# The second norm's weight multiplied into the weights' rows, with a reordered queue

## The chip, the cores and the metric

The kernel runs as one program on one core of one Trainium2 chip. The metric is the device time of the whole program in microseconds; it is given as the median of several runs. The change is compared with the kernel before it, on the same inputs.

## The reference

The input x has 32 batches of 128 channels by 512 positions; ctx has the same shape.

```
x = x + tanh(g_xattn) * cross_attention(layernorm(x), ctx, Wq, bq, Wk, bk, Wv, bv)   # 8 heads of 16
x = x + tanh(g_ffn)   * ffn(layernorm(x))

ffn(x):  h = rmsnorm(x) * rms_weight             # rms_weight: 512 values, one per feature
         probs = softmax(h @ router_w); two best of 8 experts, renormalised
         moe = sum over the two of weight * (silu(h @ w_gate) * (h @ w_up)) @ w_down
         sh  = (silu(h @ sw_gate) * (h @ sw_up)) @ sw_down
         return moe + sh
```

A batch's 128 rows of 512 are its 128 tokens in the second part. rms_weight meets h only in products over the 512 features: the router's, and the gate and up products of the eight experts and of the shared one.

## The kernel before, in words

**First part, attention, in turns.** `TURNS` runs from -3 to 31. Each engine has its own list of the turns' work, written out by hand, and within a turn TensorE, VectorE and ScalarE work through 32 slots (`STEPS`). In turn i the exponentials of batch i are made (TensorE: `exp_scores`, line 878; ScalarE: `exponential`, line 1395; TensorE: `values`, line 907), and beside them the maxima of batch i+1 (TensorE: `max_scores`, line 857; VectorE: `maximum`, line 1123, two matmuls' results to one reduction of 1.2 us). The maxima of half a batch are turned by TensorE (`turn_maxima`, line 866), taken by VectorE (`maxima_rows`, lines 1132 and 1133) and written by a DMA into one row of the q stack (`row`, line 531), from which the scores of `exp_scores` take them. The first scores of a batch need the row of half 0, its scores from slot 16 on the row of half 1.

Products of q and k are made from three bf16 parts each. ScalarE makes the high part, GpSimd the middle and low one (`split`, lines 677 to 680); SyncE writes each part to DRAM (`write`, line 456, DMAs to `parts_k` and `parts_q`) and reads them back stacked (`read`, line 470, six DMAs for each of k and q). The maxima of batch i+2 need both reads, made in turn i.

The values' result carries the denominators. Per turn, SyncE spreads them (line 486), stores the result (479), VectorE inverts them (`invert`, line 1115, in slot `RECIP_AT` = 11), SyncE stores the reciprocals (490) and, when these have landed, loads both spread out again (`load_values`, 497 and 498), and GpSimd adds the attention to x (`add_attention`, 687 to 689).

GpSimd then normalises the batch for the second part (`tokens`, line 717: scale and shift; line 718: times `w_rms`, the norm's weight broadcast to 128 partitions) and SyncE stores it to DRAM. TensorE turns it and makes the router's logits; VectorE chooses the experts; GpSimd scatters token numbers to a map by indirect DMA (`scatter`, line 733).

In turns -2 to 27 one of 30 rows of expert weights is staged per turn: loaded (`load_staged`), its high part rounded by ScalarE (`staged_high`, line 1417), its low part made by GpSimd (`staged_low`, line 725), both stored (`store_staged`). Rows 0 to 3 of an expert (or of the shared one) are gate and up weights of 128 features each, rows 4 and 5 down weights.

SyncE's order in one turn: write high q part, row of half 1, denominators, result, read k, write q parts, store reciprocals, load ctx, store turned tokens, row of half 0, read q, load values, store tokens, load x, store staged, load staged, write the three k parts. A wait in it holds all that follows.

**Second part, jobs.** From about 931 us on, 32 jobs of the shared expert and 71 routed jobs (128 gathered tokens each) run, each of which TensorE does as three products of high and low parts (line 950). Rows of the shared expert are split by VectorE in the last turn (`shared_parts`, lines 1217 and 1218), those of experts 0 to 2 beside the jobs (`placed_high`, line 1453; `placed_low`, line 1301).

Lines 1526 to 1532 set up the arrays; the rms weight is passed (line 1530) as one row of 512.

Of the kernel before, what the change touches and what calls it, by code (L numbers as in the profile page):

```python
# [15 lines left out]
P = 128  # L16
HEADS = 8
DH = P // HEADS
L = 512
# [46 lines left out]
RECIP_AT = 11  # L66
# [39 lines left out]
def build(nc, x_d, ctx_d, g_xattn_d, g_ffn_d, wq_d, bq_d, wk_d, bk_d, wv_d, bv_d, rms_d, router_d, w_d, out_d):  # L106
# [6 lines left out]
    with es:  # L113
# [62 lines left out]
        w_rms = a.take(L)  # L176

        routed_act = [w_rms[:, n * FF:(n + 1) * FF] for n in range(2)]
# [50 lines left out]
        w_router = sb("w_router", [P, CHUNKS, EXPERTS])  # L229
        before = sb("before", [P, P], BF16)  # L230
# [166 lines left out]
        n_const = 4  # L397
# [18 lines left out]
        def _(sp):  # L416
# [28 lines left out]
            load(wv[:], wv_d)  # L445
            for b in range(1, X_AHEAD - 3):
                load_x(b)
# [86 lines left out]
            for i in TURNS:  # L534
# [11 lines left out]
                if is_b(i - 1):  # L546
                    store_reciprocals(i - 1)
                if is_b(i + 4) and i + 4 >= 2:
                    load_ctx(i + 4)
                if is_b(i - 3):  # L550
                    store_turned(i - 3)
                if is_b(i + 1):
                    row(i + 1, 0)
                if is_b(i + 2):
                    read(i + 2, 1)
# [4 lines left out]
                if is_b(i + X_AHEAD):  # L560
                    load_x(i + X_AHEAD)
                if 0 <= i + 2 < len(STAGED):
                    store_staged(i + 2)
                if 0 <= i + 3 < len(STAGED):
                    load_staged(i + 3)
                if is_b(i + 3):
                    for part in (HI, MID, LO):
                        write(i + 3, 0, part)
# [12 lines left out]
                if i == 0:  # L581
                    sp.dma_start(w_router[:], router_d.rearrange("(c p) e -> p c e", p=P)).then_inc(s_wnorm, DMA)
                    sp.dma_start(w_rms, rms_d.broadcast_to([P, L])).then_inc(s_wnorm, DMA)
# [57 lines left out]
        def _(pool):  # L641
# [64 lines left out]
            def tokens(b):  # L706
# [5 lines left out]
                if b:  # L712
                    pool.wait_ge(s_tr, b)
                    pool.wait_ge(s_hst, DMA * (b + 1))
                else:
                    pool.wait_ge(s_wnorm, 2 * DMA)
                link(nc.gpsimd.tensor_scalar(tok, xs[:, b, :], r, nmr2[:, b:b + 1], ALU.mult, ALU.add))
                nc.gpsimd.tensor_tensor(tok, tok, w_rms, ALU.mult).then_inc(s_h, 1)
                pool.wait_ge(s_h, b + 1)

            def staged_low(k):
                pool.wait_ge(s_sh, k + 1)
                if k:
                    pool.wait_ge(s_sst, 2 * DMA * k)
                nc.gpsimd.tensor_tensor(staged[LOW][:], staged_raw, staged[HI][:].bitcast(F32), ALU.subtract
                                        ).then_inc(s_sl, 1)
# [19 lines left out]
            for i in TURNS:  # L746
# [6 lines left out]
                if 0 <= i + 2 < len(STAGED):  # L753
                    staged_low(i + 2)
                for b in range(B - 2 * CHUNK):
                    if i == min(b + 10, B - 1):
                        scatter(b)
                if is_b(i + 3) and i + 3 > 0:
# [52 lines left out]
        def _(pe):  # L811
# [174 lines left out]
            for i in TURNS:  # L986
                for s in range(0, STEPS, GROUP):
# [12 lines left out]
                    if is_b(i):  # L1000
                        exp_scores(i, s + 2)
                        exp_scores(i, s + 3)
                    if s == 0 and is_b(i - 1):
# [3 lines left out]
                    if s + 3 == MAX_AT[1] and is_b(i):  # L1007
                        turn_maxima(i, 1)
                    if s + 3 == MAX_AT[0] and is_b(i + 1):
                        turn_maxima(i + 1, 0)  # L1010
# [28 lines left out]
        def _(dve):  # L1039
# [172 lines left out]
            def shared_parts(r):  # L1212
                dve.wait_ge(s_wsh, W_ROWS * DMA)
                if r == 0:
                    dve.wait_ge(s_part, 4 * B)
                return chain(
# [82 lines left out]
            def placed_low(e, r):  # L1299
                dve.wait_ge(s_ph, W_ROWS * e + r + 1)  # L1300
                nc.vector.tensor_tensor(w_ring[:, e, LOW, r, :], raw_expert[:, r, :], w_ring[:, e, HI, r, :].bitcast(F32),
                                        ALU.subtract).then_inc(s_wrt, 1)
# [66 lines left out]
        def _(act_e):  # L1369
# [42 lines left out]
            def staged_high(k):  # L1412
# [4 lines left out]
                nc.scalar.copy(staged[HI][:], staged_raw).then_inc(s_sh, 1)  # L1417
# [30 lines left out]
            def placed_high(e, r):  # L1448
# [4 lines left out]
                nc.scalar.copy(w_ring[:, e, HI, r, :], raw_expert[:, r, :]).then_inc(s_ph, 1)  # L1453
# [87 lines left out]
```

## Time and profile before

| | |
|---|---|
| median of 3 runs | 1432.28 us |
| lowest, highest | 1427.72, 1443.97 us |
| the profiled execution | 1418.35 us, its span 1416.5 us |
| mean granted TensorE clock in it | 0.979 of full speed |
| busy in it: PE, VectorE, ScalarE, GpSimd | 1333.9, 984.4, 872.6, 868.1 us |
| DMA | 247.90 MB, mean 175 GB/s |

PE is TensorE, DVE is VectorE, ACT ScalarE, POOL GpSimd, SP or SPq SyncE and its queue. Instructions run one after the other on each engine; "idle before" is the time that an engine stood still ahead of an instruction, and the name behind the arrow is what it then waited for. A line stands for a place in the kernel. In order of time, a row gives start, length, engine, line, operation, what is written from what, the count, and in brackets the idle time.

### The profile page before, as it was taken

The numbers are of one execution on the slowest core, as the hardware profiler recorded it, in microseconds if no ns is written. First come the engines' busy times: TensorE is split into PE (matmuls) and PEld (weight loads), VectorE is DVE, ScalarE is ACT, GpSimd is POOL, SyncE is SP. The second block draws the span as 40 slices with busy tenths as digits, with TensorE's granted clock in tenths as the row PEclk, the third lists the DMA queues.
The fourth block names the chain that finished last, engine by engine and source line by source line (L and its number), as shares of the span: only waits on it lengthen the run. The fifth ranks groups of instructions, "written<-read, shape, count | busy, mean of one in ns | idle before, by whom it ended". The sixth has DMA issues, their size and how long they took to land.

```text
span 1416.5 us, 24632 instructions
## 1 busy us (share of the span) xinstructions
PE 1333.9 (94%) x7290; PEld 648.6 (46%) x7290; DVE 984.4 (69%) x1661; ACT 872.6 (62%) x1720; POOL 868.1 (61%) x1278
## 2 busy tenths in 40 slices
PE   3899999999999999999999998899999999999997
PEld 1222223222222322222232232377787888888886
DVE  4888889998798988988899988556654333333332
ACT  2488788788687877777787886724334333333433
POOL 7447667768687877777788864542213555555553
PEclk8799999999999999999999999999999999999999
DMA  6567676676676767676766763366554788786655
GB/s 174 159 183 220 188 215 210 187 208 198 170 192 196 200 180 193 214 182 178 200 205 188 196 181 104 101 218 154 136 186 81 195 217 207 175 198 110 114 106 81
DMA packets 161309, 247.90 MB, mean 175 GB/s; under 512 B 33605, under 2 KB 58828, under 8 KB 161182
## 3 DMA queue, kind: packets, MB, share of 16 engines
q1 hardware_dynamic: 142926, 208.96, 51.6%
q0 software_dynamic: 18256, 37.38, 14.2%
q8 instruction: 64, 1.05, 0.3%
q14 instruction: 63, 0.52, 0.1%
HBM read 141.32 MB, written 103.88 MB: 173 GB/s over the span
## 4 chain that ended last, share of the span: by engine, by line
PE 61%; DVE 13%; issue 10%; DMA 6%; SPq 4%; POOL 3%; POOLq 1%; ACT 1%; DVEq 0%; ACTq 0%
PE m_banks L950 20%; PE bank L907 12%; PE bank L878 11%; DVE row_max L1123 9%; PE m_banks L857 7%; PE bank L838 4%; PE bank L894 2%; DMA arena<-parts_q 2%; DMA arena<-arena 2%; PE bank L883 2%; PE bank L842 2%; POOL xs L781 2%; SPq L470 2%; SPq L531 1%; PE bank L972 1%
## 5 line engine op out<-in xcount | busy, mean ns | idle before, releaser
L1123 DVE TENSOR_REDUCE row_max<-m_banks 128x2 f32<-128x1024 f32 x512 | 614.6, 1222 | 68.9 <-PE m_banks L857 63.5
L1395 ACT ACTIVATE arena<-bank 128x512 f32<-128x512 f32 x1024 | 556.2, 606 | 101.7 <-PE bank L878 96.9
L878 PE MATMUL bank<-arena 112*128 112x512 bf16 x1024 | 314.8, 386 | 2.4 <-ACT arena L1395 1.5
L907 PE MATMUL bank<-arena 128*32 128x512 f32 x2048 | 277.3, 613 | 0.4 <-ACT arena L1403 0.4
L793 POOL DMA_INDIRECT out<-xs,ids x71 | 112.5, 1584 | 172.9 <-ACT xs L1470 137.9
L857 PE MATMUL m_banks<-arena 48*128 48x512 bf16 x1024 | 169.9, 393 | 47.1 <-DVE row_max L1123 34.6
L878 PEld LDWEIGHTS bank<-arena 112*128 112x128 bf16 x1024 | 79.7, 100 | 247.0 <-ACT arena L1395 88.5
L950 PE MATMUL m_banks<-w_ring,h_hi 128*128 x568 | 183.1, 403 | 0.0
L1459 ACT ACTIVATE arena<-m_banks 128x256 f32<-128x256 f32 x103 | 39.5, 384 | 188.7 <-PE m_banks L950 188.6
L857 PEld LDWEIGHTS m_banks<-arena 48*128 48x128 bf16 x1024 | 39.8, 93 | 185.2 <-issue 87.2
L950 PE MATMUL m_banks<-w_ring,h_lo 128*128 x284 | 111.7, 393 | 0.0
L1319 DVE TENSOR_TENSOR arena<-arena,m_banks 128x256 f32<-128x256 f32 x71 | 29.9, 421 | 117.0 <-ACT arena L1459 117.0
L677 POOL TENSOR_TENSOR arena<-arena 128x512 bf16<-128x512 f32 x62 | 71.8, 1157 | 63.5 <-ACT arena L1387 60.4
L950 PEld LDWEIGHTS m_banks<-w_ring,h_hi 128*128 128x128 f32 x568 | 101.4, 189 | 18.4
L687 POOL TENSOR_TENSOR arena<-arena 128x512 f32<-128x512 f32 x32 | 40.7, 1272 | 98.5 <-DMA arena<-pv_d 95.5
L1313 DVE TENSOR_TENSOR act_lo<-bank,act_hi 128x256 fp32r<-128x256 f32 x71 | 30.1, 424 | 96.7 <-ACT act_hi L1476 96.7
L781 POOL DMA_INDIRECT xs<-h_d,ids x71 | 69.7, 982 | 41.4 <-issue 21.0
L733 POOL DMA_INDIRECT map_d<-meta,slots x64 | 66.4, 1038 | 44.6 <-DVE slots L1210 28.3
L838 PE MATMUL bank<-arena 128*128 128x512 f32 x128 | 76.9, 684 | 16.8 <-POOL arena L668 12.0
L1470 ACT ACTIVATE xs<-m_banks,wts 128x512 f32<-128x512 f32 x71 | 48.8, 688 | 71.1 <-PE m_banks L950 71.1
L1378 ACT ACTIVATE arena<-bank,bias 128x512 f32<-128x512 f32 x64 | 44.0, 687 | 76.7 <-PE bank L838 76.7
L950 PE MATMUL m_banks<-w_ring,act_hi 128*128 x284 | 87.6, 390 | 1.4 <-DVE act_lo L1313 1.4
(176 smaller groups left out, 2047.9 us busy)
## 6 DMA issues: line engine op xcount, KB each, us to landing
pv_d<-arena SPq DMA_DIRECT2D x32, 512.0 KB, 4.3
w_ring<-split_d SPq DMA_DIRECT2D x60, 256.0 KB, 3.9
parts_k<-arena SPq DMA_DIRECT2D x96, 128.0 KB
parts_q<-arena SPq DMA_DIRECT2D x96, 128.0 KB
arena<-parts_k SPq DMA_DIRECT2D x64, 192.0 KB
arena<-parts_q SPq DMA_DIRECT2D x64, 192.0 KB
arena<-in_w SPq DMA_DIRECT2D x36, 256.0 KB, 7.0
arena<-in_ctx SPq DMA_DIRECT2D x32, 256.0 KB, 3.4
```

The source lines that it names most:

```text
L677: nc.gpsimd.tensor_tensor(mid, proj[n], hi, ALU.subtract).then_inc(s_part, 1)
L733: nc.gpsimd.indirect_dma_start(map_d, bass.IndirectOffsetOnAxis(ap=slots[:, k, b:b + 1], axis=0), meta[:, k, b, :], None).then_inc(s_sc2, DMA)
L781: nc.gpsimd.indirect_dma_start(gathered[i % IN_RING], None, h_d, bass.IndirectOffsetOnAxis(ap=ids[:, i:i + 1], axis=0)).then_inc(s_got[i % ...
L793: nc.gpsimd.indirect_dma_start(out_d, bass.IndirectOffsetOnAxis(ap=ids[:, i:i + 1], axis=0), y_sb[i % OUT_RING], None, compute_op=ALU.add) ...
L838: nc.tensor.matmul(out, (wk, wq)[n][:], ctx_in[b % 2] if n == 0 else xn[b % 2], start=True, stop=True).then_inc(s_proj, 1)
L857: nc.tensor.matmul(m_ps[pair % M_PAIRS][:, a, :], q_stack[b % 3][rows, h, qt * P:(qt + 1) * P], k_stack[b % 3][rows, h, :], start=True, st ...
L878: nc.tensor.matmul(out, k_stack[b % 3][0:SHIFTED, h, kt * P:(kt + 1) * P], q_stack[b % 3][0:SHIFTED, h, :], start=True, stop=True).then_in ...
L907: last = nc.tensor.matmul(pv_ps[2 * DH * j:2 * DH * (j + 1), :], v_ones[b % 3][:, kt, GROUP * g + j, :], probs[pair % 3][:, j, :], start=( ...
L950: last = nc.tensor.matmul(out, v[:, c, :], weights(j, part, first_row + c), start=(c == 0 and n == 0), stop=(c == chunks - 1 and n == 2))
L1123: nc.vector.reduce_max(pair, m_ps[(STEPS * b + u) // 2 % M_PAIRS], AX_X).then_inc(s_mx, 1)
L1395: nc.scalar.activation(probs[group % 3][:, j, :], bank_of["scores", b, s], ACT.Exp, scale=float(DH) ** -0.5).then_inc(s_exp, 1)
L1470: nc.scalar.activation(y_sb[i % OUT_RING], Y_PS[j % 2], ACT.Copy, scale=wts[:, i:i + 1]).then_inc(s_yrt, 1)
```

## The change

The norm's weight is loaded at the start as 128 x 4 values, feature by partition, in place of a broadcast of 512 to all partitions in turn 0. GpSimd no longer multiplies the tokens by it; it multiplies the router's weights once. The gate and up rows (0 to 3) get the factor where their high and low parts are made: staged rows by ScalarE (a multiply in place of a copy) and GpSimd (one more instruction, in place, ahead of the subtraction), shared and placed rows in forms of the same instructions with a second operand. Rows 4 and 5 are as before. So the tokens in DRAM are without the weight.

Beside it the order changes. On SyncE the read of q goes ahead of the store of reciprocals and of the row of half 0, and the high k part is written ahead of the staged parts. On GpSimd the scatters go ahead of the staged low part. On TensorE `turn_maxima` goes ahead of `values` in its slots. On VectorE the reciprocals move from slot 11 to slot 16.

```diff
--- before.py
+++ after.py
@@ -63,7 +63,7 @@
 LOGITS_AT = 16
 MOMENTS2_AT = 10
 MOMENTS_AT = 27
-RECIP_AT = 11
+RECIP_AT = 16
 GROUP = 4
 EXPERTS = 8
 FF = 256
@@ -173,9 +173,7 @@
         added_all = a.take(NT + 1)
         a.take(2 * L - NT * EXPERTS - NT - 1)
         assert a.at >= attention_end, (a.at, attention_end)
-        w_rms = a.take(L)
-
-        routed_act = [w_rms[:, n * FF:(n + 1) * FF] for n in range(2)]
+        routed_act = [a.take(FF) for _ in range(2)]
 
 
 
@@ -227,6 +225,7 @@
         nmr2 = sb("nmr2", [P, B])
         newton = sb("newton", [P, 1])
         w_router = sb("w_router", [P, CHUNKS, EXPERTS])
+        w_rms = sb("w_rms", [P, CHUNKS])
         before = sb("before", [P, P], BF16)
         ones = sb("ones", [P, P], BF16)
         route = sb("route", [P, 12 * C])
@@ -394,7 +393,7 @@
         MOMENTS_JOB = 6
         TURN_AT = 24
 
-        n_const = 4
+        n_const = 5
         TURNS = range(-3, B)
 
         ROUTER_JOBS = {0: B - 3, 4: B - 2, 9: B - 1}
@@ -443,6 +442,7 @@
             load(gates[:, 0:1], g_xattn_d.broadcast_to([P, 1]))
             load(gates[:, 1:2], g_ffn_d.broadcast_to([P, 1]))
             load(wv[:], wv_d)
+            load(w_rms[:], rms_d)
             for b in range(1, X_AHEAD - 3):
                 load_x(b)
 
@@ -543,29 +543,31 @@
                     read(i + 2, 0)
                     write(i + 2, 1, MID)
                     write(i + 2, 1, LO)
-                if is_b(i - 1):
-                    store_reciprocals(i - 1)
                 if is_b(i + 4) and i + 4 >= 2:
                     load_ctx(i + 4)
                 if is_b(i - 3):
                     store_turned(i - 3)
+                if is_b(i + 2):
+                    read(i + 2, 1)
+                if is_b(i - 1):
+                    store_reciprocals(i - 1)
                 if is_b(i + 1):
                     row(i + 1, 0)
-                if is_b(i + 2):
-                    read(i + 2, 1)
                 if is_b(i - 1):
                     load_values(i - 1)
                 if is_b(i - 2):
                     store_tokens(i - 2)
                 if is_b(i + X_AHEAD):
                     load_x(i + X_AHEAD)
+                if is_b(i + 3):
+                    write(i + 3, 0, HI)
                 if 0 <= i + 2 < len(STAGED):
                     store_staged(i + 2)
                 if 0 <= i + 3 < len(STAGED):
                     load_staged(i + 3)
                 if is_b(i + 3):
-                    for part in (HI, MID, LO):
-                        write(i + 3, 0, part)
+                    write(i + 3, 0, MID)
+                    write(i + 3, 0, LO)
                 for r in SHARED_ROWS.get(i, ()):
                     if r == 2:
                         sp.wait_ge(s_sst, 2 * DMA * len(STAGED))
@@ -580,7 +582,6 @@
                     sp.dma_start(map_tiles[EXPERTS * B:], unused_map).then_inc(s_map0, DMA)
                 if i == 0:
                     sp.dma_start(w_router[:], router_d.rearrange("(c p) e -> p c e", p=P)).then_inc(s_wnorm, DMA)
-                    sp.dma_start(w_rms, rms_d.broadcast_to([P, L])).then_inc(s_wnorm, DMA)
 
 
             def load_expert(e, r):
@@ -713,15 +714,20 @@
                     pool.wait_ge(s_tr, b)
                     pool.wait_ge(s_hst, DMA * (b + 1))
                 else:
-                    pool.wait_ge(s_wnorm, 2 * DMA)
-                link(nc.gpsimd.tensor_scalar(tok, xs[:, b, :], r, nmr2[:, b:b + 1], ALU.mult, ALU.add))
-                nc.gpsimd.tensor_tensor(tok, tok, w_rms, ALU.mult).then_inc(s_h, 1)
+                    pool.wait_ge(s_wnorm, DMA)
+                    pool.wait_ge(s_const, n_const * DMA)
+                    link(nc.gpsimd.tensor_tensor(w_router[:], w_router[:],
+                                                 w_rms[:].unsqueeze(2).broadcast_to([P, CHUNKS, EXPERTS]), ALU.mult))
+                nc.gpsimd.tensor_scalar(tok, xs[:, b, :], r, nmr2[:, b:b + 1], ALU.mult, ALU.add).then_inc(s_h, 1)
                 pool.wait_ge(s_h, b + 1)
 
             def staged_low(k):
                 pool.wait_ge(s_sh, k + 1)
                 if k:
                     pool.wait_ge(s_sst, 2 * DMA * k)
+                r = STAGED[k][1]
+                if r < CHUNKS:
+                    link(nc.gpsimd.tensor_scalar(staged_raw, staged_raw, w_rms[:, r:r + 1], None, ALU.mult))
                 nc.gpsimd.tensor_tensor(staged[LOW][:], staged_raw, staged[HI][:].bitcast(F32), ALU.subtract
                                         ).then_inc(s_sl, 1)
 
@@ -750,11 +756,11 @@
                     normalise(i + 4)
                 if is_b(i - 2):
                     tokens(i - 2)
-                if 0 <= i + 2 < len(STAGED):
-                    staged_low(i + 2)
                 for b in range(B - 2 * CHUNK):
                     if i == min(b + 10, B - 1):
                         scatter(b)
+                if 0 <= i + 2 < len(STAGED):
+                    staged_low(i + 2)
                 if is_b(i + 3) and i + 3 > 0:
                     split(i + 3, 0)
                 if is_b(i - 1):
@@ -1000,14 +1006,14 @@
                     if is_b(i):
                         exp_scores(i, s + 2)
                         exp_scores(i, s + 3)
+                    if s + 3 == MAX_AT[1] and is_b(i):
+                        turn_maxima(i, 1)
+                    if s + 3 == MAX_AT[0] and is_b(i + 1):
+                        turn_maxima(i + 1, 0)
                     if s == 0 and is_b(i - 1):
                         values(i - 1, STEPS // GROUP - 1)
                     if s and is_b(i):
                         values(i, s // GROUP - 1)
-                    if s + 3 == MAX_AT[1] and is_b(i):
-                        turn_maxima(i, 1)
-                    if s + 3 == MAX_AT[0] and is_b(i + 1):
-                        turn_maxima(i + 1, 0)
                     if s + 3 == COUNT_SLOT and i >= 7 and (i - 7) % CHUNK == 0:
                         count_choices((i - 7) // CHUNK)
                     if i == B - 1 and s == FIRST_JOB_AT:
@@ -1213,6 +1219,13 @@
                 dve.wait_ge(s_wsh, W_ROWS * DMA)
                 if r == 0:
                     dve.wait_ge(s_part, 4 * B)
+                if r < CHUNKS:
+                    return chain(
+                        lambda: nc.vector.tensor_scalar(shared_hi[:, r, :], w_shared[:, r, :], w_rms[:, r:r + 1], None,
+                                                        ALU.mult),
+                        lambda: nc.vector.scalar_tensor_tensor(shared_lo[:, r, :], w_shared[:, r, :], w_rms[:, r:r + 1],
+                                                               shared_hi[:, r, :].bitcast(F32), ALU.mult, ALU.subtract
+                                                               ).then_inc(s_wsp, 1))
                 return chain(
                     lambda: nc.vector.tensor_copy(shared_hi[:, r, :], w_shared[:, r, :]),
                     lambda: nc.vector.tensor_tensor(shared_lo[:, r, :], w_shared[:, r, :],
@@ -1298,8 +1311,13 @@
 
             def placed_low(e, r):
                 dve.wait_ge(s_ph, W_ROWS * e + r + 1)
-                nc.vector.tensor_tensor(w_ring[:, e, LOW, r, :], raw_expert[:, r, :], w_ring[:, e, HI, r, :].bitcast(F32),
-                                        ALU.subtract).then_inc(s_wrt, 1)
+                hi = w_ring[:, e, HI, r, :].bitcast(F32)
+                if r < CHUNKS:
+                    nc.vector.scalar_tensor_tensor(w_ring[:, e, LOW, r, :], raw_expert[:, r, :], w_rms[:, r:r + 1], hi,
+                                                   ALU.mult, ALU.subtract).then_inc(s_wrt, 1)
+                else:
+                    nc.vector.tensor_tensor(w_ring[:, e, LOW, r, :], raw_expert[:, r, :], hi, ALU.subtract
+                                            ).then_inc(s_wrt, 1)
 
             def tokens_low(j):
                 hi, lo = (flat(v) for v in tokens_of(j))
@@ -1414,7 +1432,11 @@
                 if k:
                     act_e.wait_ge(s_sl, k)
                     act_e.wait_ge(s_sst, 2 * DMA * k)
-                nc.scalar.copy(staged[HI][:], staged_raw).then_inc(s_sh, 1)
+                r = STAGED[k][1]
+                if r < CHUNKS:
+                    nc.scalar.mul(staged[HI][:], staged_raw, w_rms[:, r:r + 1]).then_inc(s_sh, 1)
+                else:
+                    nc.scalar.copy(staged[HI][:], staged_raw).then_inc(s_sh, 1)
 
             def exponentials(c):
                 act_e.wait_ge(s_ch, c + 1)
@@ -1450,7 +1472,10 @@
                     act_e.wait_ge(s_praw, DMA * W_ROWS * (e + 1))
                 if e == IN_PLACE - 1:
                     act_e.wait_ge(s_dn, B)
-                nc.scalar.copy(w_ring[:, e, HI, r, :], raw_expert[:, r, :]).then_inc(s_ph, 1)
+                if r < CHUNKS:
+                    nc.scalar.mul(w_ring[:, e, HI, r, :], raw_expert[:, r, :], w_rms[:, r:r + 1]).then_inc(s_ph, 1)
+                else:
+                    nc.scalar.copy(w_ring[:, e, HI, r, :], raw_expert[:, r, :]).then_inc(s_ph, 1)
 
             def silu(j):
                 act_e.wait_ge(s_gu, j + 1)
@@ -1527,7 +1552,7 @@
     arrays = dict(
         x=x, ctx=inputs["ctx_2048"], g_xattn=inputs["g_xattn"].reshape(1, 1), g_ffn=inputs["g_ffn"].reshape(1, 1),
         wq=attention("Wq").T, bq=attention("bq").reshape(P, 1), wk=attention("Wk").T, bk=attention("bk").reshape(P, 1),
-        wv=attention("Wv").T, bv=attention("bv").reshape(P, 1), rms=ffn("rms_weight").reshape(1, L),
+        wv=attention("Wv").T, bv=attention("bv").reshape(P, 1), rms=ffn("rms_weight").reshape(CHUNKS, P).T,
         router=ffn("router_w"), w=weights.transpose(0, 2, 1, 3))
     arrays = {f"in_{name}": np.ascontiguousarray(value) for name, value in arrays.items()}
     tokens = x.shape[0] * P
```

## Rows read from the trace of the kernel before

**Rows 1.** Busy by stage: PE, PEld, DVE, ACT, POOL; clock, DMA share, GB/s.

```profile
110.00:890.00 780.00, 745.99 (x4409) 218.87 (x4408) 683.92 (x1070) 609.78 (x1171) 570.50 (x953) 0.99 0.68 191
890.00:931.00 41.00, 34.82 (x186) 17.18 (x184) 22.64 (x60) 24.06 (x47) 23.41 (x36) 0.96 0.41 125
1060.00:1416.00 356.00, 346.40 (x1727) 287.01 (x1725) 114.94 (x225) 133.91 (x293) 177.43 (x137) 0.99 0.69 148
```

**Rows 2.** The page, the chain that ended last, by engine.

```profile
PE 61%; DVE 13%; issue 10%; DMA 6%; SPq 4%; POOL 3%; POOLq 1%; ACT 1%; DVEq 0%; ACTq 0%
```

**Rows 3.** Busy time by engine in single turns, columns as in the first group.

```profile
537.20:564.80 27.60, 26.00 (x159) 7.68 (x155) 23.78 (x40) 21.42 (x42) 21.53 (x37) 1.00 0.71 193
730.80:756.80 26.00, 25.69 (x159) 7.79 (x155) 24.16 (x39) 21.35 (x42) 21.11 (x36) 1.00 0.72 208
```

**Rows 4.** Waits of TensorE from 53 to 890 us: total, times, longest.

```profile
PE m_banks L857 <- DVE row_max L1123: 28.4, 47, 1.4
PE m_banks L857 <- DMA arena<-parts_q: 6.0, 4, 2.1
```

**Rows 5.** Waits of VectorE from 53 to 890 us.

```profile
DVE m_rows L1132 <- PE bank L866: 14.6, 30, 1.5
DVE arena L1115 <- issue: 13.7, 8, 2.7
DVE arena L1115 <- DVE stats L1088: 2.4, 4, 1.0
```

**Rows 6.** Chain of waits, 545 to 553 us: start, length, what.

```profile
543.10 3.56 DMA arena<-arena
546.66 1.77 issue
```

**Rows 7.** TensorE in order of time, two instructions of two turns.

```profile
551.65 0.39 PE L857 MATMUL m_banks<-arena 48*128 48x512 bf16 x2 [1.12 <-DVE row_max L1123]
425.83 0.60 PE L878 MATMUL bank<-arena 112*128 112x512 bf16 x2
```

**Rows 8.** Waits of SyncE's queue from 53 to 890 us.

```profile
SPq L531 <- DVE m_rows L1133: 101.6, 58, 6.2
```

**Rows 9.** Chain of waits at the start, issue to landing.

```profile
21.60 3.83 DMA parts_q<-arena
50.68 4.18 DMA arena<-parts_q
```

**Rows 10.** SyncE's queue in order of time, parts of two turns.

```profile
413.44 1.33 SPq L456 DMA_DIRECT2D parts_q<-arena  x2
...
416.37 1.22 SPq L531 DMA_DIRECT2D arena<-m_rows  x2
418.08 3.76 SPq L470 DMA_DIRECT2D arena<-parts_q  x6
421.95 0.63 SPq L497 DMA_DIRECT2D arena<-rden_d  x1
...
435.38 3.81 SPq L470 DMA_DIRECT2D arena<-parts_k  x6
...
774.67 3.77 SPq L470 DMA_DIRECT2D arena<-parts_q  x6
...
790.32 3.80 SPq L470 DMA_DIRECT2D arena<-parts_k  x6
```

**Rows 11.** GpSimd by line, 110 to 890 us: busy, mean ns, idle before.

```profile
L718 POOL TENSOR_TENSOR arena<-arena 128x512 f32<-128x512 f32 x29 | 37.1, 1280 | 2.4
L687 POOL TENSOR_TENSOR arena<-arena 128x512 f32<-128x512 f32 x29 | 36.9, 1271 | 79.8 <-DMA arena<-pv_d 79.8
L717 POOL TENSOR_SCALAR arena<-xs,r,nmr 128x512 f32<-128x512 f32 x29 | 22.4, 774 | 2.9
```

**Rows 12.** The store of reciprocals, line 490, to landing.

```profile
DMA to landing us min/median/max: 1.4/3.1/4.2
```

**Rows 13.** One group of ScalarE by line, 110 to 890 us.

```profile
L1417 ACT CAST staged_hi<-arena 128x512 fp32r<-128x512 f32 x26 | 16.3, 629 | 0.0
```

## The prediction

> **What bounds the kernel now.** I read the view by stages first. From 110 to 890 us the attention turns run: TensorE is busy 746.0 of 780 us, VectorE 683.9, ScalarE 609.8, GpSimd 570.5; from 1060 us on, in the routed jobs, TensorE is busy 346.4 of 356 us and nobody else is near [rows 1]. The chain that ended last says the same: PE 61%, DVE 13% [rows 2]. The change touches nothing that TensorE computes, so it can only win TensorE's idle time, and of that there are some 34 us in the turns and 10 us behind them. A turn takes 780/29 = 26.9 us on average (29 is the count of line 687, once a turn [rows 11]).
>
> Next, single turns. One without a stall takes 26.0 us with TensorE busy 25.7; one with a stall takes 27.6 with TensorE busy 26.0 [rows 3]. The list of waits names the two causes: TensorE waits 28.4 us (47 times) in the maxima's matmuls for VectorE's reductions and 6.0 us (4 times) for the reads of the q parts [rows 4]. VectorE's own waits, one level deeper: 13.7 + 2.4 us (12 times) before the reciprocal of line 1115 and 14.6 us (30 times) before line 1132, which takes the turned maxima [rows 5]. The chain of one stalled turn shows the link: the denominators are in flight for 3.56 us, VectorE waits 1.77 us in front of its reciprocal, and TensorE then idles 1.12 us for the reduction queued behind it [rows 6, 7]. So of such a wait 1.12/1.77 = 0.63 reaches TensorE.
>
> Last, SyncE's queue, because the change mostly permutes it. It waits 101.6 us (58 times) for the rows of maxima [rows 8], with the reads of the q parts queued behind.
>
> **The change, part by part.**
>
> Reciprocal moved from slot 11 to 16 of VectorE's order: 16.1 us of waiting go, worth 16.1 x 0.63 = 10 us. Bounds: 0 (the reductions wait for TensorE anyway) and 16. The stores that need it were moved behind the reads, so its lateness costs nothing.
>
> Turning of maxima ahead of the value products on TensorE: the transpose runs about 1 us sooner (a group of value products), so VectorE's 14.6 us before line 1132 go. VectorE then mostly meets the next wait for TensorE, so I take 3 us; bounds 0 and 14.6 x 0.63 = 9. The value products start 0.28 us later; their reader on ScalarE comes a slot later.
>
> Reads of the q parts ahead of reciprocals and rows: their data are there earlier. The last q part is issued at about 414.1 (second of the pair at 413.44), and such a write lands 3.83 us after issue [rows 9], at 417.9; the reads start at 418.08, behind the rows issued at 416.37 [rows 10]. In the turn at 790.32 the pair is issued from 794.2 on, that is 790.32 + 3.80, and would have landed by 798.7, while the waits for maxima [rows 8] hold the queue 1 to 2 us. The 6.0 us of TensorE's waits for these reads should go: 5 us; bounds 0 and 6. Sum of these three: 10 + 3 + 5 = 18 us off, if nothing else becomes late.
>
> GpSimd: line 718 goes, 1.28 us a turn; one tensor_scalar like line 717, 0.77 us, comes for four of six staged rows [rows 11]. Net 0.4 us less per such turn, 1.3 otherwise. Worth nothing: GpSimd already idles 79.8 us before line 687 waiting for the loaded values [rows 11], and this cover stays. Scatters ahead of the staged part: the store of the staged low half may be 2 us later, but SyncE gets there later too. ScalarE multiplying in place of copying, 0.63 us each [rows 13]: at worst the few hundredths of a scale operand, and ScalarE is idle 170 us of 780 [rows 1]. The shared rows' two-operand forms on VectorE: a few tenths each, four times, in a stretch where it is busy 22.6 of 41 us [rows 1]. The placed rows: VectorE and ScalarE are busy under 40% of the routed jobs [rows 1]. Weight load: one small issue moved to the start behind wv and the x of batch 0, a broadcast gone later: nothing. One 128x32 multiply on GpSimd, once: nothing.
>
> **What the permuted queue costs.** The store of reciprocals now follows the six reads, and loading values waits for that store. The store of tokens, the load of x, the first k part and the staged parts stand behind that wait; GpSimd's addition of attention, and later ScalarE's staged row in slot 15, wait for what they bring. Before, values were issued 3.87 us after the reads began (421.95 against 418.08 [rows 10]), their bytes queued behind the reads' without a gap. Now follow one lap of the queue's own loop. The six reads take 3.8 us to issue and the last lands 4.18 us after its issue [rows 9]: all landed at +7.4. The reciprocals, issued at +3.9, pass behind them: taken as landed with the reads at +7.4. Then load_values is issued, and the DMA engines have run dry: a gap of 1.4 us, the smallest time to landing of this store [rows 12], for I found no purer row; bounds 0.5 and its median 3.1. Then the burst (values, tokens, x, staged halves, weights, k parts), until the k parts have landed and their reads start: from 418.08 + 7.4 = 425.5 to 435.38, 9.9 us, and from 774.67 + 7.4 to 790.32, 8.2 us [rows 10]; I take 9.1. Then the six k reads (3.8), the two q parts (issue of the last at +0.7) and its landing (3.83): 8.35. Sum 7.4 + 1.4 + 9.1 + 8.35 = 26.3 us; bounds 24.5 and 28.8. TensorE without the 18 us would turn in 26.9 - 18/29 = 26.3 us. A tie: each turn takes the later of two paces that both vary, so I take 26.6, that is 0.3 x 29 = 9 us of the 18 given back. The first wait to show it would be the first row of maxima of a batch: issued behind reads, reciprocals and at +4.5 it lands about +7.5 to +8.5, while in the tight turn the scores need it 7.75 us after the reads begin (425.83 [rows 7] against 418.08 [rows 10]).
>
> The Trainium skill (DMA: Bandwidth & Descriptors, "Queues, rings and completion order") says that one issuer's descriptors are taken in ring order and that the semaphore increment lands only after every earlier write of that DMA engine. By that rule a small store behind six reads cannot signal before them, which speaks against this order; with its page's fixed 2 us in place of 1.4 the lap would be 26.9, an estimate by that page. The trace neither contradicts nor isolates it.
>
> **Rivals.** (a) TensorE alone sets the pace: the lap closes in 26 us or less (shorter gap, or the burst at 8.2), and all 18 us stay, perhaps 22 with more of line 1132. Time 1432 - 20 = 1412. For it: the k reads already wait at the queue, so the burst may fill in; half of the staged traffic is unchanged. Chance 0.36. (b) Slower: the reciprocals' store behind the reads delays load_values by 2 us and more each turn; the lap becomes 27.6 (midway from 26.3 to the upper bound 28.8), SyncE's late row of maxima stops TensorE before the first scores of each turn, +0.7 x 29 = +20 us, 1452. It decides once the lap passes 27.4 (26.9 and 14 us spread over 29 turns). For it: DMA engines are busy 0.7 of these turns [rows 3], the tight turn has 0.3 us of slack. Chance 0.22. (c) The stall only moves: VectorE now waits in front of line 1088 for x that GpSimd adds after the later values, and nothing changes: 1430, part of the forecast's side.
>
> **How the numbers follow.** The profiled execution took 1418.35 us (span 1416.5); the runs shown have median 1432.28 (1427.72 to 1443.97), so it lies 1% below them. My forecast, -9 us, gives 1409 against its own time and 1423 against the median, which is the number I give. What a measurement of this kernel can tell from no change is about 1%, 14 us. Forecast with (c): 0.42, all of it within 1%. Faster by over 1%: (a), 0.36. Slower by over 1%: (b), 0.22. The forecast's own range is 1418 to 1436, the lap between 26.1 and 26.8 and (c). The whole range reaches down to 1404, which is (a) with bounds of its terms (16 + 6 + 6 = 28 us off), and up to 1450, about (b)'s middle; what is left out is the upper half of (b), up to 1487 where the lap is at its bound of 28.8 ((28.8 - 26.9) x 29 = 55 us), and a small tail of (a), together under 2 in 10.
>
> **What would show it.** Right: no idle before line 1115 (now 12 waits) and next to none before 1132; no wait of TensorE for the q parts; SyncE's wait for maxima much shorter and a new wait for the reciprocals' store in front of load_values of 1.5 to 2.5 us a turn; unstalled turns at 26.3 to 26.6. (a) if turns are 26.0 to 26.3. (b) if TensorE's line 878 waits for the DMA of m_rows. Wrong altogether if the routed jobs, 346.4 us of TensorE, change, since nothing there should.

## The result, and the profile after

Slower: 1487.72 us median (1480.6 to 1490.2, 4 runs) against 1430.0 (1426.54 to 1443.97, 4 runs), ratio 1.038, 95% interval 1.030 to 1.046. The profiled execution took 1480.6 us, span 1478.7, with a mean granted TensorE clock of 0.964 (before 0.979). I had forecast 1423 and a range up to 1450. What came is the second rival, and the time at the bound that the prediction had left out (1487, for a lap of 28.8 us; the laps in the trace are longer, see below).

The page's chain that ended last, by engine, where PE and DVE stood first before [rows 2]:

```profile
DMA 32%; SPq 26%; PE 23%; issue 10%; POOL 3%; DVE 3%; ACT 1%; POOLq 1%; ACTq 0%
```

So on this chain SyncE's queue and the transfers that it waits for come first. Line numbers have shifted: in the kernel after, `exp_scores` is line 884, `max_scores` 863, `maximum` 1129, `invert` 1121, `add_attention` 688; SyncE's 470 to 531 are as before. First the stages, columns as in [rows 1]; the second row is the same stretch of routed jobs, reckoned from the end:

```profile
110.00:890.00 780.00, 715.43 (x4097) 203.11 (x4093) 628.01 (x998) 574.27 (x1093) 535.10 (x903) 0.96 0.63 180
1122.00:1478.00 356.00, 345.33 (x1717) 285.10 (x1715) 114.00 (x222) 133.83 (x291) 177.46 (x137) 1.00 0.69 148
```

The routed jobs are untouched (345.3 of 356 us, before 346.4 [rows 1]). The loss lies in the turns: TensorE's busy time in 780 us fell from 746.0 to 715.4, its clock from 0.99 to 0.96, the share of the DMA engines from 0.68 to 0.63. All engines do less per microsecond. Both windows lie inside the turns, which end some 60 us later than before.

The waits of TensorE from 53 to 890 us (total, times, longest), to be held against [rows 4]:

```profile
PE bank L884 <- DMA arena<-m_rows: 52.2, 35, 4.2
PE m_banks L863 <- DVE row_max L1129: 10.4, 33, 1.0
```

The waits that the change aimed at did shrink: for VectorE's reductions from 28.4 to 10.4 us, for the q parts from 6.0 to none. A new one is larger than both: the scores wait for the row of maxima. VectorE (against [rows 5]) no longer waits before the reciprocal or before the turned maxima, but it waits for its inputs and, a little, for x:

```profile
DVE row_max L1129 <- PE m_banks L863: 129.5, 143, 5.3
DVE stats L1094 <- POOL xs L690: 16.4, 15, 1.8
```

And SyncE's queue in the same stretch (against [rows 8]):

```profile
SPq L497 <- DMA rden_d<-arena: 75.9, 27, 4.7
SPq L470 <- DMA parts_q<-arena: 57.6, 29, 2.4
SPq L470 <- DMA parts_k<-arena: 44.6, 26, 2.3
```

Its wait for the rows of maxima, 101.6 us before, is down to 1.2: the rows are ready when SyncE comes to them, because SyncE comes late. In its place stands a wait of 2.8 us a turn at line 497, `load_values`, for the reciprocals' store. SyncE's waits for engines are 4 us in all now, beside 178 us for transfers: the queue waits for its own DMAs.

One lap in order of time (start, length, line, what, count), against [rows 10]:

```profile
407.21 3.77 SPq L470 DMA_DIRECT2D arena<-parts_q  x6
411.02 0.59 SPq L490 DMA_DIRECT2D rden_d<-arena  x1
411.66 1.18 SPq L531 DMA_DIRECT2D arena<-m_rows  x2
415.71 0.66 SPq L497 DMA_DIRECT2D arena<-rden_d  x1
...
420.90 1.25 SPq L456 DMA_DIRECT2D parts_k<-arena  x2
...
427.95 3.81 SPq L470 DMA_DIRECT2D arena<-parts_k  x6
431.80 1.33 SPq L456 DMA_DIRECT2D parts_q<-arena  x2
...
436.05 1.23 SPq L470 DMA_DIRECT2D arena<-parts_q  x2
```

From one set of q reads to the next it is 436.05 - 407.21 = 28.8 us. The store is issued 3.8 us after the reads begin, and 4.7 us pass before `load_values` may go, at +8.5; before it went at +3.9 [rows 10]. The two rows of maxima, issued from 411.66 on, are under way behind the reads, and TensorE stands:

```profile
416.93 0.86 PE L884 MATMUL bank<-arena 112*128 112x512 bf16 x2 [2.71 <-DMA arena<-m_rows]
```

The lap shown is shorter than most. Over the 23 laps from batch 6 on, start of q reads to start of q reads, the mean is 29.5 us, against 27.2 before: 2.3 x 29 turns = 65 us, and the spans differ by 62. Split into the same three stretches (26 laps that begin between 110 and 870 us), the means are 8.9 us to `load_values`, at most 10.4, then 12.3 to the k reads and 8.3 to the next q reads.

### The profile page after: what moved, and what is told of

Same layout as the page of the kernel before. It is cut to its first block, busy times and chain, and to the rows that moved or that the text cites. A ratio compares the mean times of both kernels' runs of the same rounds, so it can differ in the third digit from the quotient of the medians.

```text
span 1478.7 us, 24638 instructions
## 1 busy us (share of the span) xinstructions
PE 1361.0 (92%) x7290; PEld 646.5 (44%) x7290; DVE 975.4 (66%) x1661; ACT 881.0 (60%) x1720; POOL 855.5 (58%) x1267
## 4 chain that ended last, share of the span: by engine, by line
DMA 32%; SPq 26%; PE 23%; issue 10%; POOL 3%; DVE 3%; ACT 1%; POOLq 1%; ACTq 0%
PE m_banks L956 17%; SPq L470 15%; DMA parts_k<-arena 12%; DMA rden_d<-arena 10%; DMA parts_q<-arena 7%; SPq L456 4%; SPq L520 2%; POOL xs L787 2%; DMA out<-xs,ids 2%; DVE row_max L1129 2%; SPq L497 1%; PE bank L913 1%; SPq L514 1%; SPq L498 1%; PE bank L889 1%
## 5 line engine op out<-in xcount | busy, mean ns | idle before, releaser
L884 PE MATMUL bank<-arena 112*128 112x512 bf16 x1024 | 321.4, 396 | 55.9 <-DMA arena<-m_rows 53.6
L913 PE MATMUL bank<-arena 128*32 128x512 f32 x2048 | 282.2, 623 | 0.3 <-ACT arena L1421 0.3
L884 PEld LDWEIGHTS bank<-arena 112*128 112x128 bf16 x1024 | 72.4, 101 | 363.0 <-ACT arena L1413 138.8
L863 PE MATMUL m_banks<-arena 48*128 48x512 bf16 x1024 | 174.4, 402 | 27.2 <-DVE row_max L1129 21.0
L1331 DVE TENSOR_TENSOR act_lo<-bank,act_hi 128x256 fp32r<-128x256 f32 x71 | 30.1, 424 | 96.5 <-ACT act_hi L1501 96.5
L844 PE MATMUL bank<-arena 128*128 128x512 f32 x128 | 77.3, 688 | 17.0 <-POOL arena L669 12.3
```

The lines of the kernel that those rows point to most:

```text
L844: nc.tensor.matmul(out, (wk, wq)[n][:], ctx_in[b % 2] if n == 0 else xn[b % 2], start=True, stop=True).then_inc(s_proj, 1)
L863: nc.tensor.matmul(m_ps[pair % M_PAIRS][:, a, :], q_stack[b % 3][rows, h, qt * P:(qt + 1) * P], k_stack[b % 3][rows, h, :], start=True, st ...
L884: nc.tensor.matmul(out, k_stack[b % 3][0:SHIFTED, h, kt * P:(kt + 1) * P], q_stack[b % 3][0:SHIFTED, h, :], start=True, stop=True).then_in ...
L913: last = nc.tensor.matmul(pv_ps[2 * DH * j:2 * DH * (j + 1), :], v_ones[b % 3][:, kt, GROUP * g + j, :], probs[pair % 3][:, j, :], start=( ...
```

## The experiments

The fold is the norm's weight multiplied into the weights' rows. Theory L: SyncE's lap, lengthened by the reciprocals' store behind the reads, is the whole loss. Rival R: the row of maxima behind the reads stops TensorE. Rival F: the fold costs. The runs come in three sets of four, in the order below, each on another chip. All ratios are against the kernel before on the same chip, where it took 1449.87, 1445.56 and 1447.4 us, with a 95% interval in brackets. No trace of the kernel before belongs to these sets: its rows are of the execution of 1418.35 us. Where a wait of a run is held against [rows 4], [rows 5] or [rows 8], a part of the difference can be the chip's.

**The fold alone.**

```diff
 after.py, with all orders and RECIP_AT = 11 as before
```

> The weight goes into the weights' rows as in the changed kernel; all orders (SyncE, GpSimd, TensorE, slot 11 of the reciprocals) are those of before. Theory L (the lap of SyncE's queue, lengthened by the reciprocals' store behind the reads, is the whole loss): 0 to 4 us under before, 1426 to 1430, turns of 26.9 us. Rival F (the folding itself costs, through ScalarE's multiplies, GpSimd's extra instruction or VectorE's two-operand forms): 1450 or more.

Measured 1.003 (0.999 to 1.007), 1450.42 us. The fold is free within what can be told; it wins nothing either, as costed. F falls. This kernel has VectorE's order of before, and shows more waiting ahead of the reciprocal than [rows 5], 30.4 us in place of 16.1 (53 to 890 us):

```profile
DVE arena L1119 <- issue: 22.8, 13, 3.4
DVE arena L1119 <- DMA arena<-arena: 4.3, 2, 2.2
DVE arena L1119 <- DVE stats L1092: 3.3, 6, 0.8
```

**The reordering alone.**

```diff
 before.py, with SyncE's, GpSimd's and TensorE's orders of after and
-RECIP_AT = 11
+RECIP_AT = 16
```

> The reordering alone, tokens multiplied by the weight as before. Theory L: the whole loss is here, ratio 1.03 to 1.045 (1475 to 1492), SyncE waits 75 to 90 us for the reciprocals' store ahead of line 497's like. Rival F: near before.

Measured 1.030 (1.022 to 1.038), 1492.14 us; SyncE waits 79.6 us at line 497 from 53 to 890 us (86.4 up to 950). The loss is in the order.

**The changed kernel, the store put back.**

```diff
+                if is_b(i - 1):
+                    store_reciprocals(i - 1)
                 if is_b(i + 4) and i + 4 >= 2:
                     load_ctx(i + 4)
 ...
                 if is_b(i + 2):
                     read(i + 2, 1)
-                if is_b(i - 1):
-                    store_reciprocals(i - 1)
                 if is_b(i + 1):
                     row(i + 1, 0)
```

> The changed kernel with one step undone: the store of reciprocals goes back ahead of the load of ctx; the row of half 0 stays behind the reads of q. Theory L: load_values is issued 5.1 us after the reads begin in place of 8.5 to 9.5, the lap falls from 29.5 to about 26.7, time 1420 to 1436, and TensorE's wait for the rows of maxima falls under 10 us. Rival R (it is the row of maxima behind the six reads that stops TensorE): TensorE still waits about 50 us for m_rows and the time stays over 1465.

Measured 0.998 (0.994 to 1.002), 1445.69 us. This one step takes back the whole loss; of the 18 us that were to be won nothing is seen clear of noise, and the lap is 28.2 us in the mean, not 26.7. TensorE still waits 22.6 us for rows of maxima (53 to 950 us), more than the 10 that I had written, less than half of R's 50. SyncE now waits for the reciprocal itself (53 to 890 us):

```profile
SPq L490 <- DVE arena L1121: 58.1, 27, 3.6
SPq L531 <- DVE m_rows L1139: 52.5, 26, 4.1
```

**The changed kernel, the row put back.**

```diff
+                if is_b(i + 1):
+                    row(i + 1, 0)
                 if is_b(i + 2):
                     read(i + 2, 1)
                 if is_b(i - 1):
                     store_reciprocals(i - 1)
-                if is_b(i + 1):
-                    row(i + 1, 0)
```

> The changed kernel with the other step undone: the row of half 0 goes back ahead of the reads of q; the store of reciprocals stays behind them. Theory L: load_values still waits for that store, the lap stays at 28.8 to 30, time 1475 to 1500, with TensorE's waits for m_rows replaced by waits for the q reads. Rival R: the row is in time, the waits are gone, 1445 or less.

Measured 1.042 (1.034 to 1.051), 1511.77 us. R said 1445 or less, and falls. My detail was off: TensorE's waits for rows did not vanish (line 884 from 53 to 950 us), they moved:

```profile
PE bank L884 <- DMA arena<-m_rows: 40.2, 21, 3.8
PE m_banks L863 <- DMA arena<-parts_q: 19.1, 13, 3.3
```

Counted by slot, all 40 us now lie before slot 16, that is before the row of half 1, which SyncE issues early in the next turn; in the changed kernel 46 of 53 us (53 to 950 us) lay before slot 0, the row of half 0. With the row moved forward TensorE waits for another row and for q parts, and the loss stays: where it waits is a symptom of the late queue.

**Slot 16 alone, in the kernel before.**

```diff
-RECIP_AT = 11
+RECIP_AT = 16
```

> The kernel before with the reciprocals in slot 16 of VectorE's order and nothing else. The prediction's term of 10 us: ratio 0.993 or less if SyncE, which now waits for the reciprocal ahead of its store, does so only in time that it spent on the next row of maxima anyway. Rival (seen in the run with the store put back, where SyncE waited 69 us there): that wait delays the reads of q, TensorE then waits for them, ratio 1.00 or above. VectorE's idle time before the reciprocal goes to 0 in both.

Measured 0.981 (0.975 to 0.986), 1419.28 us against 1445.56. This is the lowest ratio of the study, below the kernel before and the changed one: some 27 us (20 to 36 by the interval) for one number. The wait that could have eaten it is there, 29.1 us (18 times) at SyncE's line 490 from 53 to 890 us, and seems to lie in time that SyncE spent on the maxima before (50.5 us left of 101.6 [rows 8]). TensorE's waits for the q parts, the expectation's rival, are 12.2 us (6 times), against 6.0 [rows 4]. VectorE's list from 53 to 890 us has no reciprocal any more (against [rows 5]):

```profile
DVE row_max L1123 <- PE m_banks L857: 69.2, 154, 4.6
DVE m_rows L1132 <- PE bank L866: 8.6, 30, 1.3
DVE stats L1088 <- POOL xs L689: 3.7, 3, 1.6
```

**turn_maxima first, in the kernel before.**

```diff
+                    if s + 3 == MAX_AT[1] and is_b(i):
+                        turn_maxima(i, 1)
+                    if s + 3 == MAX_AT[0] and is_b(i + 1):
+                        turn_maxima(i + 1, 0)
                     if s == 0 and is_b(i - 1):
                         values(i - 1, STEPS // GROUP - 1)
 ...
```

> The kernel before with turn_maxima ahead of values on TensorE and nothing else. The prediction's term of 3 us, bounds 0 and 9: ratio 0.994 to 1.000, VectorE's idle time before line 1132 gone. Rival: TensorE waits for a free bank of scores with the transpose in front, ratio above 1.000.

Measured 0.988 (0.982 to 0.994), 1429.74 us: about 17 us, more than the term of 3 us; the interval, 9 to 26 us, begins at the term's bound of 9. VectorE's wait before 1132 is out of its list.

**The changed kernel with SyncE's order of before.**

```diff
 SyncE's order of before.py (reads, rows, stores, k parts); all else as after.py
```

> The changed kernel with SyncE's whole order put back to that of before; the fold, slot 16, turn_maxima first and GpSimd's order stay. Theory L: no lap over TensorE's pace, so no loss: ratio 0.985 to 1.000, no wait of TensorE for m_rows. Rival (some other part of the change shares the loss): 1.01 or more.

Measured 0.994 (0.990 to 0.998), 1438.83 us. No loss without the queue's order; but less gain than slot 16 has alone. TensorE waits 24.8 us (13 times, 53 to 890 us) for the q parts.

**The changed kernel with the staged transfers last.**

```diff
-                if is_b(i + 3):
-                    write(i + 3, 0, HI)
+                if is_b(i + 3):
+                    for part in (HI, MID, LO):
+                        write(i + 3, 0, part)
                 if 0 <= i + 2 < len(STAGED):
                     store_staged(i + 2)
                 if 0 <= i + 3 < len(STAGED):
                     load_staged(i + 3)
-                if is_b(i + 3):
-                    write(i + 3, 0, MID)
-                    write(i + 3, 0, LO)
```

> The changed kernel with all three k parts written ahead of the staged stores and load; the reciprocals' store stays behind the reads. Theory L as a lap of DMA time: 768 KB leave the stretch between load_values and the landing of the k parts, at some 200 GB/s 3 us or more of the 12.3, so the lap falls from 29.5 to 26 to 27 us although the reciprocals' store is as late as ever: ratio 0.99 to 1.01 against before. Rival P (what costs is the wait for the reciprocals' landing as such, through GpSimd's addition or the late row, at any length of the lap): ratio stays over 1.025.

Measured 1.019 (1.013 to 1.025), 1473.68 us, between what L and P had said. About half of the loss is gone although the store lands as late as ever (`load_values` goes 9.0 us after the reads in the mean, 8.9 in the changed kernel), which speaks against P as the whole cause; but the lap shrank less than I wrote, to 29.1 us in the mean, so L's figure of 26 to 27 failed too. The queue in order of time shows why:

```profile
410.29 0.66 SPq L497 DMA_DIRECT2D arena<-rden_d  x1
...
417.92 1.22 SPq L531 DMA_DIRECT2D arena<-m_rows  x2
419.24 1.26 SPq L486 DMA_DIRECT2D arena<-arena  x2
420.60 0.40 SPq L479 DMA_DIRECT2D pv_d<-arena  x1
421.10 3.87 SPq L470 DMA_DIRECT2D arena<-parts_k  x6
```

The k reads no longer wait for the k parts: 16 issues between 410.29 and 421.00 fill the time from `load_values` to the k reads, 10.8 us against 12.2 in the changed kernel (means 11.1 and 12.3). Below the DMAs' time lies the issuing time of the queue.

**Both VectorE-side gains together.**

```diff
-RECIP_AT = 11
+RECIP_AT = 16
 and turn_maxima ahead of values, in before.py
```

> The kernel before with slot 16 for the reciprocals and turn_maxima ahead of values, SyncE's and GpSimd's orders and the tokens' multiply as before: the candidate that should beat both. The two gains measured alone were 0.981 and 0.988. If they are independent: 0.970; if both feed the same slack of VectorE: 0.978 to 0.985, since TensorE's idle time in the turns is all there is to win.

Measured 0.986 (0.981 to 0.991), 1426.27 us. They do not add up: 0.970 was what independent gains would have given. The two together are no better than slot 16 alone (0.981, measured in the set before).

**Slot 16 and the fold.**

```diff
 the fold alone (above), and
-RECIP_AT = 11
+RECIP_AT = 16
```

> Slot 16 and the fold of the weight, all orders of before. The kernel with SyncE's order put back gained only 0.6% where slot 16 alone gained 1.9%. If the fold takes the rest: 0.990 to 0.995. If it is GpSimd's order or the two edits together: 0.980 to 0.984.

Measured 0.987 (0.981 to 0.993), 1428.71 us. Its interval overlaps that of slot 16 alone; whether the fold takes back half a per cent stays open. TensorE's waits for the q parts are 24.1 us here (53 to 890 us), as in the kernel with SyncE's order put back (24.8), against 12.2 with slot 16 alone. The fold's longer work on GpSimd, which makes q parts too, is a possible reason; no run tried it.

**Slot 16, and the store alone behind the reads.**

```diff
-                if is_b(i - 1):
-                    store_reciprocals(i - 1)
                 if is_b(i + 4) and i + 4 >= 2:
 ...
                 if is_b(i + 2):
                     read(i + 2, 1)
+                if is_b(i - 1):
+                    store_reciprocals(i - 1)
                 if is_b(i - 1):
                     load_values(i - 1)
```

> Slot 16 and one more edit: the store of reciprocals goes behind the reads of q (the row of maxima stays ahead of them), nothing folded. Theory L: this one move makes the loss, SyncE waits over 80 us for its landing, lap over 29 us, ratio 1.02 to 1.045 against before. Rival R (the row's place decides): 0.98 to 1.00.

Measured 1.044 (1.038 to 1.050), 1509.62 us. Against slot 16 alone (0.981) this one moved DMA costs 6.3%, about 90 us; against the next run, of the same set, 77 us. SyncE's waits and TensorE's from 53 to 950 us (69.4 us of the first up to 890 us, less than the 80 that L had said):

```profile
SPq L497 <- DMA rden_d<-arena: 80.9, 22, 6.8
SPq L470 <- DMA parts_k<-arena: 57.6, 27, 3.2
SPq L531 <- DVE m_rows L1133: 37.6, 19, 4.6
```

```profile
PE bank L878 <- DMA arena<-m_rows: 47.0, 26, 4.6
PE m_banks L857 <- DVE row_max L1123: 19.8, 49, 1.4
```

The lap by stretches, in the mean between 110 and 870 us: `load_values` goes 8.0 us after the reads (4.0 with slot 16 alone), and the rest takes 22.1 us (23.1), 30.1 in place of 27.1. The run is also slower than the reordering with everything in it (1.030): with the store behind the reads, the row ahead of them makes it worse, as in the run with the row put back (1.042).

**Slot 16, and the row alone behind the reads.**

```diff
-                if is_b(i + 1):
-                    row(i + 1, 0)
                 if is_b(i + 2):
                     read(i + 2, 1)
+                if is_b(i + 1):
+                    row(i + 1, 0)
```

> Slot 16 and the other edit alone: the row of half 0 goes behind the reads of q, the store stays ahead. Theory L: load_values goes out 5.2 us after the reads begin, the lap stays within TensorE's pace, ratio 0.98 to 1.00, with at most some 20 us of waits for the row at the first scores. Rival R: 1.02 or more.

Measured 0.989 (0.984 to 0.994), 1433.01 us. `load_values` goes 5.2 us after the reads, as written, and waits for nothing; TensorE's waits for rows from 53 to 950 us:

```profile
PE bank L878 <- DMA arena<-m_rows: 21.1, 19, 2.7
```

Against slot 16 alone (0.981) the row's move costs 0.8%, some 12 us, with intervals that just overlap. The other two kernels of this set with slot 16, turn_maxima first and the fold, lie at 0.986 and 0.987, and slot 16 alone was not run in this set, so a part of the 12 us may be a difference between the sets. Beside the store's 77 to 90 us it is small either way.

## Why the prediction was wrong

**The step that failed** is the lap's sum, "Sum 7.4 + 1.4 + 9.1 + 8.35 = 26.3 us; bounds 24.5 and 28.8". The mechanism was the right one, and it decides the sign, as the pair of store behind (1.044) and row behind (0.989) shows; two terms were mis-sized, both to the same side. First the lap of 28.8 us shown above, means in brackets:
- *The reciprocals "taken as landed with the reads at +7.4".* SyncE goes on at +8.5 (407.21 to 415.71; mean 8.9). In the view of line 490 the time to landing has the median 4.9 us, before 3.1 [rows 12]:

```profile
DMA to landing us min/median/max: 1.4/4.9/6.6
```

- *Gap 1.4 and burst 9.1, together 10.5.* From `load_values` to the k reads 12.2 us passed (415.71 to 427.95; mean 12.3). The term reckoned with DMA time alone. The staged-last run shows 10.8 us of issues without a break in this stretch, already more than 10.5; in the changed kernel SyncE waits for k parts beside (44.6 us in 26 turns, 1.7 a turn). And the burst was not as short as the stretch before the change: there the burst's first transfers were queued while the reads still ran, and I had subtracted the reads' whole time, as if nothing of the burst had been served in it. That this overlap belongs to the missing 1.7 us is an argument, not shown by a run.
- The last term, 8.35, was right: 8.1 (427.95 to 436.05; mean 8.3).

8.5 + 12.2 + 8.1 = 28.8, the upper bound of my sum; in the mean 29.4 to 29.5, beyond it. The pace that I held it against was off too: 780/29 = 26.9 took the number of additions in a window for the number of turns, and the laps before are 27.2 us. So the loss is 2.3 us a turn, where the bound had 1.9, and that 1487.72 us came so close to the 1487 of the bound is luck. I had called middle values the likely ones for terms that the same cause, a fuller queue, pushes up together.

**The Trainium skill's rule.** That a small store behind six reads cannot signal before them (DMA: Bandwidth & Descriptors, "Queues, rings and completion order") agrees with the trace: 4.9 us to landing in the median in place of 3.1. When the reads themselves landed no row shows. I cited it as speaking against the order and then let the lap tie. The 2 us that stand beside it in the prediction are on that page under "Anatomy of one DMA — SWDGE (gpsimd) path", for a DMA that GpSimd issues; this store is SyncE's, and the sum did not use the figure.

**Reciprocal in slot 16**, 10 us with bounds 0 and 16: alone it is worth about 27. Which factor was too low is not settled. The 16.1 us were read from an execution of 1418.35 us; the fold-only kernel, 1448.83 us in its profiled execution and with the same order on VectorE, waits 30.4 us there, and 30.4 x 0.63 would be 19. The 0.63 comes from one stalled turn; late reductions also set when maxima are turned and so when SyncE's queue moves on. That this is the route was not tested by itself.

**turn_maxima first**, 3 us, bounds 0 and 9: alone some 17, and together with slot 16 nothing more. That looks like one slack, counted by me in two terms.

**Reads of q earlier**: TensorE's 6.0 us of waits for them are gone, as said; but SyncE itself now waits 57.6 us for the q parts ahead of these reads.

**GpSimd's and ScalarE's parts at nothing**: right in effect (fold alone 1.003), wrong in size. ScalarE's multiply takes 0.10 us more than the copy, not a few hundredths, and GpSimd's added line twice what I took (last section). The difference from line 718 was misreckoned besides: 1.28 - 0.77 is 0.5, not 0.4.

**What would show it** had named the sign of the case that came: "if TensorE's line 878 waits for the DMA of m_rows". It does, 52.2 us; that was the symptom. The wait of SyncE at line 497, named there as a mark of the forecast's case at 1.5 to 2.5 us a turn, is 2.8. The rival had the mechanism and the sign right, but its middle, 1452, was too low by 36.

**The 18 us.** Without the late store they do not come either: the two kernels that keep all else and have the store back ahead of the reads gain 0.2% and 0.6% (0.998 and 0.994), some 3 and 9 us. The three gains were added as if they were independent.

**The clock.** TensorE's granted clock was 0.96 in the turns against 0.99 [rows 1], and 0.94 from 407 to 436 us. There pairs of score matmuls took 0.86 and 1.04 us right behind the 2.71 us of standing quoted above, and 0.60 from 421.18 us on. With the lap bound by DMAs and issues, how much of the 62 us the clock adds was not separated.

## What to carry to other kernels

A hand-written DMA queue is a loop: add up one lap, from landing to landing and with the issuing time beside it, before moving anything in it, and take the mean of many laps, not one. In this kernel a small store whose landing the same queue waits for did not bear being put behind large transfers: what got earlier by it was worth far less than the wait that is paid in every lap. And an engine that waits in its order for something not yet needed (here one reciprocal in slot 11) is worth a look first: moving it five slots later, alone, gave 1.9%.

## What the runs showed of the hardware

GpSimd's tensor_scalar on 128x512 float32 takes twice as long in the added form (one factor from a pointer, no second operation, in place) as line 717's form with two operations, 0.77 us [rows 11]; ScalarE's multiply by a pointer takes 0.73 us, the copy 0.63 [rows 13]. The two added lines, median in the middle:

```profile
L730 POOL TENSOR_SCALAR arena<-arena,w_rms x20: 1557/1570/1603, 28.3 to 804.5; 128x512 f32<-128x512 f32 x20
```

```profile
L1437 ACT ACTIVATE staged_hi<-arena,w_rms x20: 722/732/733, 17.2 to 794.4; 128x512 fp32r<-128x512 f32 x20
```

So in the turns of staged rows 0 to 3 GpSimd does 0.3 us more than before (1.57 against 1.28), where I had reckoned less. Which of the three differences in form makes it slow was not tried.

Issuing takes SyncE time of its own: in the lap of 28.8 us shown above its 35 DMAs take 0.33 to 0.67 us each, 20.7 us in all, and in the staged-last run 16 issues fill 10.8 us.
